# Moving VectorE's low half of the attention output from behind the last row maximum to behind the first shift of the scores

## The chip, the cores and the metric

The kernel runs on one core of a Trainium2 chip. The metric is the device time of one execution in microseconds (us), as a median over runs. The core has five engines that run beside each other, each with a queue of its own that it works off in order: TensorE (PE: matmuls, and their weight loads, shown as PEld), VectorE (DVE), ScalarE (ACT), GpSimd (POOL) and SyncE (SP, which issues DMAs). They wait for each other through semaphores.

## The reference

`x` has shape (4, 1024, 256), the context (4, 77, 256). Four layers follow each other, each added to `x`:

```python
x = x + cross_attention_0(layernorm(x), ctx)        # softmax(q k^T / 4) v, 16 heads of 16, biases
x = x + ffn_sine(layernorm(x))                      # 256 -> 1024 -> 256, sine transform, relu
x = x + cross_attention_1(ctx, layernorm(x), mask)  # the same, scores masked where mask == 0
x = x + ffn_fp4(layernorm(x))                       # gate, up, down with blockwise FP4 rounding
```

One attention, for a tile of 128 rows of `x`:

```python
q = layernorm(x) @ Wq + bq                     # (128, 256)
s = einsum(q, k)                               # (128, 16 heads, 77 keys)
p = exp((s - rowmax(s)) * scale)               # row maximum of each head
o = (p @ v) / sum(p)                           # (128, 256)
x = x + o @ Wo + bo
```

## The kernel before

The 4 x 1024 rows are T = 32 tiles of 128 rows. `attention` runs for layer l = 0 (the first attention) and l = 1 (the second), with an FFN behind each. Each attention is a software pipeline over steps i = -3 to 33, written out by hand: every engine has a function `step(i, u)` that lists its instructions for several tiles at once, and the order of these lines is the engine's order. Semaphore waits (`wait(...)`) tie the engines together. In step i the work on tile t is at these stages:

- tile i+1: layernorm result transposed (TensorE, `psQ`), copied (ScalarE, L675), query product (L753), its high half written by ScalarE (L693), its low half by VectorE (L567);
- tile i: scores (TensorE, L736, into four PSUM banks `psS[0..3]`), row maxima of each bank (`row_max`, L503), and the subtraction of the maximum (`shift`, L511);
- tile i-1: the shifted scores are transposed on TensorE in three groups of 4, 4 and 2 blocks into the one bank `psT` (L792). ScalarE takes the exponential of each group (L686). A group may overwrite `psT` only when the exponential of the group before it has ended (`prob_ready`). Then the product with the values (L814);
- tile i-2: reciprocal of the denominators (L494) and normalised output `on` (L497) on VectorE, transposed on TensorE into `psY` (`attended`, L745), high half of it rounded and copied by ScalarE (`attended_high`, L667), low half (`psY` minus the high half) by VectorE, and then the output projection on TensorE (`projected`, L762), which waits for the low half (`oT_low`). The residual (L521) adds it to `x`.

The projection multiplies split numbers, a high and a low half of both operands, so the low half `oTs[:, u, 1, :]` is needed before its first product.

TensorE's order inside a step is: scores of tile i, transposes of tile i+1, transposes of `on` of tile i-2, first group of shifted scores, query product, second group, `projected`, third group, product with the values. ScalarE's order is: copy of the transposed layernorm result (L675), `attended_high` (L667), first exponential, high half of the queries (L693), second exponential, third exponential.

In steps 5 to 28 of the first attention VectorE and GpSimd also prepare one piece of the FP4 weights of the last layer (`w4_scales`, `w4_powers`: L381 to L411 on VectorE, L400 to L424 on GpSimd). There are 24 such steps, and the second attention has none; it has instead four more matmuls per step that put the mask into the scores (L729). In step 4 of the first attention VectorE also computes small coefficients.

The line that the change moves is the low half in VectorE's `step`:

```python
wait(dve, oT_high, i - 1)
nc.vector.tensor_tensor(oTs[:, u, 1, :], psY[:, 0:KC * P], oTs[:, u, 0, :].bitcast(F32),
                        ALU.subtract).then_inc(oT_low, 1)
```

Of the kernel before, what the change touches and what calls it, by code (L numbers as in the profile page):

```python
# [53 lines left out]
def valid(t, n=T):  # L54

    return not isinstance(t, int) or 0 <= t < n


def wait(eng, sem, count):

    if not isinstance(count, int) or count > 0:
        eng.wait_ge(sem, count)
# [364 lines left out]
def attention(nc, sem, l, g):  # L427
# [5 lines left out]
    with ExitStack() as ctx:  # L433
# [42 lines left out]
        def piece_of(i):  # L476

            return i - LOOP_FROM if l == 0 and LOOP_FROM <= i < LOOP_TO else None

        def quarters_of(i):  # L480

            return {1: (0,), 2: (1,), 3: (2, 3)}.get(i, ()) if l == 0 else ()
# [4 lines left out]
        with nc.Block() as block:  # L487
            @block.vector
            def _(dve):
                def outputs(t, u):  # L490

                    wait(dve, pv_mm, t + 1)
                    o = psO[:, 0:H * VW].rearrange("p (h w) -> p h w", w=VW)
                    nc.vector.reciprocal(rden[:, u, :].unsqueeze(2), o[:, :, HD:VW]).then_inc(rden_set, 1)  # L494
                    wait(dve, rden_set, t + 1)
                    wait(dve, oT_mm, t - 1)
                    nc.vector.tensor_tensor(on[:, u, :].rearrange("p (h d) -> p h d", d=HD), o[:, :, 0:HD],  # L497
                                            rden[:, u, :].unsqueeze(2).broadcast_to([P, H, HD]),
                                            ALU.mult).then_inc(on_ready, 1)

                def row_max(t, u, j):
                    wait(dve, score_mm, NB * t + j + 1)
                    nc.vector.tensor_reduce(mx[:, u, j * BH:(j + 1) * BH],  # L503
                                            psS[j][:, 0:BH * KV].rearrange("p (h k) -> p h k", k=KV),
                                            AX.X, ALU.max).then_inc(mx_set, 1)

                def shift(t, u, j):
                    wait(dve, mx_set, NB * t + j + 1)
                    if j == 0:
                        wait(dve, prob_mm, 3 * (t - 1))  # L510
                    nc.vector.tensor_tensor(  # L511
                        shifted[:, u, 0:HK].rearrange("p (c j n k) -> p j c n k", c=KC, j=NB, n=PAIR)[:, j],
                        psS[j][:, 0:BH * KV].rearrange("p (c n k) -> p c n k", c=KC, n=PAIR),
                        mx[:, u, j * BH:(j + 1) * BH].rearrange("p (c n) -> p c n", c=KC).unsqueeze(3)
                        .broadcast_to([P, KC, PAIR, KV]),
                        ALU.subtract).then_inc(shifted_ready, 1)

                def residual(t):
                    wait(dve, y_mm, t + 1)
                    wait(dve, bias_added, t + 1)  # L520
                    nc.vector.tensor_tensor(x[:, t, :], x[:, t, :], psY[:, 0:D], ALU.add).then_inc(x_done, 1)  # L521

                def normalise(t, u):
                    wait(dve, rstd_ready, t + 1)
                    wait(dve, xT_mm, t - 1)
                    nc.vector.tensor_scalar(xhat[:, u, :], x[:, t, :], mv[:, u, 0:1], rstd[:, u, :],
                                            ALU.subtract, ALU.mult).then_inc(xhat_ready, 1)

                def step(i, u):
                    v = 1 - u  # L530
                    if valid(i - 2):
                        outputs(i - 2, u)
                    if valid(i):
                        row_max(i, u, 0)
                        row_max(i, u, 1)
                        shift(i, u, 0)
                        row_max(i, u, 2)
                        shift(i, u, 1)
                        row_max(i, u, 3)
                    if valid(i - 2):  # L540

                        wait(dve, oT_high, i - 1)
                        nc.vector.tensor_tensor(oTs[:, u, 1, :], psY[:, 0:KC * P], oTs[:, u, 0, :].bitcast(F32),  # L543
                                                ALU.subtract).then_inc(oT_low, 1)
                    if valid(i):
                        shift(i, u, 2)
                        shift(i, u, 3)
                    if piece_of(i) is not None:
                        if piece_of(i) == 0:
                            dve.wait_ge(g["in_w4"], 16)  # L550
                        w4_scales(nc, dve, g, piece_of(i), u, 0)
                    if l == 0 and i + 3 == 0:
                        dve.wait_ge(g["in_xa"], 16)
                    if l == 0 and i + 3 == 2:
                        dve.wait_ge(g["in_x0"], 16)
                    if l == 0 and i + 3 == R:
                        dve.wait_ge(g["in_x"], 16 * (B - 1))
                    if valid(i + 3):
                        nc.vector.bn_stats(st[:, v, :], x[:, i + 3, :]).then_inc(st_set, 1)
                        wait(dve, st_set, i + 4)  # L560
                    if piece_of(i) is not None:
                        w4_scales(nc, dve, g, piece_of(i), u, 1)
                    if valid(i + 1):

                        wait(dve, q_high, i + 2)
                        for k in range(KC):
                            last = nc.vector.scalar_tensor_tensor(  # L567
                                qTs[:, v, 1, k, :], psQ[:, k * P:(k + 1) * P],
                                cols[:, C_BQ + 2 * l + k:C_BQ + 2 * l + k + 1], qTs[:, v, 0, k, :].bitcast(F32),
                                ALU.add, ALU.subtract)  # L570
                        last.then_inc(q_low, 1)
                    if piece_of(i) is not None:
                        w4_scales(nc, dve, g, piece_of(i), u, 2)
                    if valid(i + 2):
                        normalise(i + 2, u)
                    if piece_of(i) is not None:
                        w4_scales(nc, dve, g, piece_of(i), u, 3)
                    if valid(i + 3):
                        nc.vector.bn_aggr(mv[:, v, :], st[:, v, :]).then_inc(mv_ready, 1)  # L579
                    for n in quarters_of(i):  # L580
                        w_low_parts(nc, dve, g, n)
                    if valid(i - 2):
                        residual(i - 2)
                    if piece_of(i) is not None:
                        w4_powers(nc, dve, g, piece_of(i), u)

                nc.vector.memset(shifted[:, 0, HK:HKP], 0.0).then_inc(pad_set, 1)
                nc.vector.memset(shifted[:, 1, HK:HKP], 0.0).then_inc(pad_set, 1)
                def masks(b):
                    part = slice(b * R * KV, (b + 1) * R * KV)  # L590
                    if b == 0:
                        dve.wait_ge(g["in_mask"], 16 * B)
                    nc.vector.tensor_scalar(mb[:, part], mask[:, part], 0.0, MASKED, ALU.is_equal, ALU.mult
                                            ).then_inc(mb_set, 1)

                if inputs:
                    inputs.angles(dve)
                step(-3, 1)
                context.key_lows(dve)
                step(-2, 0)  # L600
                if inputs:
                    inputs.pair_mask(dve)
                    dve.wait_ge(g["pairmask_set"], 1)
                context.first_keys_on_vector(dve)
                context.bias_row(dve)
                if l:
                    masks(0)
                step(-1, 1)
                for i in range(0, LAST):
                    step(i, i % 2)  # L610
                    if i == 0:
                        context.values(dve)
                    if i == 1:
                        context.projection_low(dve)
                    if i == 4 and inputs:
                        inputs.coefficients(dve)
                    if l and 0 < i < B:
                        masks(i)
# [916 lines left out]
```

## Time and profile before

| | before |
|---|---|
| median of 3 runs | 1028.1 us (1027.95 to 1029.42) |
| profiled execution, its own time | 1030.46 us |
| profiled execution, span | 1028.6 us |
| TensorE clock granted, mean | 0.963 of full |

The trace is of one execution. A row of the timeline gives the start of an instruction or of a run of like instructions (us from the span's start), its duration, engine, line and tiles; the brackets at the end give the idle time of the engine in front of it and what ended that. Instructions of one engine overlap in the timeline by some 0.1 us at their borders, so the distance between two starts is the time that one takes of its engine's queue. The first attention takes about the first quarter of the span, the second lies between about 505 and 755 us.

### The profile page before, as it was taken

Reading aid. Unit: us, or ns where it says so; the run is one execution under the profiler, and the core shown is the slowest. Engines: PE = TensorE matmul, PEld = TensorE weight load, DVE = VectorE, ACT = ScalarE, POOL = GpSimd, SP = SyncE. Lnnn points to the kernel's source line nnn. Section 1 sums busy time; section 2 is a strip of 40 time slices with the busy share of each in tenths; the row PEclk is TensorE's granted clock in tenths of the full one; section 3 lists DMA queues with packets and bytes.
Section 4 is the critical chain, followed back from the end, with each engine's and each line's share of the span. In section 5 each row is a group of like instructions: output and inputs, shape, how many; then the busy total and the mean of one; then the engine's idle time right before and its main releaser. Section 6 shows DMA issues by size and latency. Waiting matters only on the chain. (4 is left out here: it accounts for less than half of the span.)

```text
span 1028.6 us, 20339 instructions
## 1 busy us (share of the span) xinstructions
PE 931.2 (91%) x7332; PEld 819.3 (80%) x7332; DVE 832.3 (81%) x2172; ACT 487.6 (47%) x1019; POOL 466.4 (45%) x663
## 2 busy tenths in 40 slices
PE   6899999998689999998899999999868999999997
PEld 5788888887578888887688888888756888888885
DVE  5799999996399999986788787777557898898874
ACT  2534334333098888886343343333334444444442
POOL 2134545541266666664211212112026777777762
PEclk9899999999599999999999999999968999999999
DMA  9020000000000000000100000000000000000000
GB/s 344 16 94 2 2 3 2 2 2 1 0 1 1 2 1 1 1 1 4 48 2 1 2 1 2 3 1 2 1 1 1 21 1 22 21 21 21 22 21 21
DMA packets 6083, 18.32 MB, mean 18 GB/s; under 512 B 864, under 2 KB 2784, under 8 KB 5472
## 3 DMA queue, kind: packets, MB, share of 16 engines
q1 hardware_dynamic: 5264, 16.52, 4.2%
q8 instruction: 59, 0.97, 0.4%
q10 hardware_dynamic: 720, 0.50, 0.2%
q14 instruction: 40, 0.33, 0.1%
HBM read 12.83 MB, written 4.19 MB: 17 GB/s over the span
## 5 line engine op out<-in xcount | busy, mean ns | idle before, releaser
L814 PE MATMUL a_psO<-vblk,a_prob 128*128 128x51 f32 (+1 forms) x1280 | 154.1, 277 | 0.0
L814 PEld LDWEIGHTS a_psO<-vblk,a_prob 128*128 128x128 f32 x1280 | 153.8, 198 | 0.0
L1407 PE MATMUL f_psGU<-wgu,f_xTs 128*128 128x512 f32 (+1 forms) x576 | 141.3, 390 | 3.8 <-ACT f_silu L1359 2.4
L503 DVE TENSOR_REDUCE a_mx<-a_psS 128x4 f32<-128x308 f32 x256 | 115.0, 470 | 23.8 <-PE a_psS L736 23.5
L686 ACT ACTIVATE a_prob<-a_psT 128x512 f32<-128x512 f32 (+1 forms) x192 | 101.1, 526 | 68.5 <-PE a_psT L792 66.5
L675 ACT COPY a_xTs<-a_psQ 128x256 f32<-128x256 f32 x64 | 23.9, 373 | 206.6 <-PE a_psQ L745 206.6
L1407 PEld LDWEIGHTS f_psGU<-wgu,f_xTs 128*128 128x128 f32 x576 | 103.7, 192 | 19.6 <-DVE f_xTs L1171 4.4
L643 POOL TENSOR_TENSOR a_rstd<-a_mv,expo 128x1 f32<-128x1 f32 x64 | 15.3, 239 | 220.3 <-DVE a_mv L579 220.2
L511 DVE TENSOR_TENSOR a_shifted<-a_psS,a_mx 128x308 f32<-128x308 f32 x256 | 114.6, 468 | 0.0
L792 PE MATMUL a_psT<-ident,a_shifted 128*128 128x128 f32 x640 | 103.4, 276 | 9.5 <-ACT a_prob L686 9.5
L1033 PEld LDWEIGHTS s_psY<-w,s_hid 128*128 128x128 f32 x768 | 97.4, 188 | 18.1 <-POOL s_hid L951 14.3
L1033 PE MATMUL s_psY<-w,s_hid 128*128 128x256 f32 x768 | 102.3, 282 | 6.7 <-POOL s_hid L951 6.5
L1021 PE MATMUL s_psH<-s_xTs,w 128*128 128x512 f32 x384 | 102.8, 405 | 2.7 <-DVE s_xTs L932 2.0
L951 POOL TENSOR_TENSOR s_hid<-wat,s_hid 128x512 fp32r<-128x512 f32 x64 | 86.1, 1347 | 39.0 <-ACT wat L988 38.9
L1424 PE MATMUL f_psY<-wdT,f_hTs 128*128 128x256 f32 x384 | 89.7, 384 | 1.6 <-ACT f_hTs L1364 1.6
L762 PE MATMUL a_psY<-wo,a_oTs 128*128 128x256 f32 x384 | 65.6, 308 | 27.7 <-DVE a_oTs L543 27.7
L762 PEld LDWEIGHTS a_psY<-wo,a_oTs 128*128 128x128 f32 x384 | 52.1, 198 | 43.1 <-DVE a_oTs L543 43.1
L792 PEld LDWEIGHTS a_psT<-ident,a_shifted 128*128 128x128 f32 x640 | 74.7, 142 | 12.1 <-ACT a_prob L686 12.1
L1424 PEld LDWEIGHTS f_psY<-wdT,f_hTs 128*128 128x128 f32 x384 | 73.6, 192 | 13.5 <-issue 1.5
L1021 PEld LDWEIGHTS s_psH<-s_xTs,w 128*128 128x128 f32 x384 | 69.5, 193 | 16.2 <-DVE s_xTs L932 2.4
L753 PE MATMUL a_psQ<-a_xTs,wat 128*128 128x128 f32 x512 | 72.7, 286 | 1.9 <-ACT a_xTs L675 1.8
L753 PEld LDWEIGHTS a_psQ<-a_xTs,wat 128*128 128x128 f32 x512 | 63.9, 196 | 4.9 <-ACT a_xTs L675 3.4
(158 smaller groups left out, 1876.2 us busy)
## 6 DMA issues: line engine op xcount, KB each, us to landing
out_x<-x SPq DMA_DIRECT2D x8, 512.0 KB, 2.6
x<-in_x SPq DMA_DIRECT2D x3, 1024.0 KB, 13.3
w<-in_w SPq DMA_DIRECT2D x1, 2304.0 KB, 9.2
w<-in_w SPq DMA_DIRECT2D x2, 1024.0 KB, 18.0
a_mask<-in_mask SPq DMA_DIRECT2D x4, 308.0 KB, 3.9
wat<-in_att SPq DMA_DIRECT2D x1, 1024.0 KB, 22.7
x<-in_x SPq DMA_DIRECT2D x1, 768.0 KB, 9.3
wat<-in_att SPq DMA_DIRECT2D x2, 256.0 KB, 5.3
```

The costliest lines, as they stand in the source:

```text
L503: nc.vector.tensor_reduce(mx[:, u, j * BH:(j + 1) * BH], psS[j][:, 0:BH * KV].rearrange("p (h k) -> p h k", k=KV), AX.X, ALU.max).then_inc ...
L511: nc.vector.tensor_tensor(shifted[:, u, 0:HK].rearrange("p (c j n k) -> p j c n k", c=KC, j=NB, n=PAIR)[:, j], psS[j][:, 0:BH * KV].rearra ...
L686: nc.scalar.activation(prob[:, v, c0 * P:c1 * P], psT[:, 0:(c1 - c0) * P], ACT.Exp, scale=scale).then_inc(prob_ready, 1)
L753: mm = nc.tensor.matmul(psQ[:, h * P:(h + 1) * P], wat[:, k, h * P:(h + 1) * P], xTs[:, u, k * P:(k + 1) * P], start=(k == 0), stop=(k == ...
L762: mm = nc.tensor.matmul(psY[:, 0:D], oTs[:, u, a, k * P:(k + 1) * P], wo[:, b, k, :], start=(m == 0), stop=(m == len(terms) - 1))
L792: mm = nc.tensor.transpose(psT[:, (c - c0) * P:(c - c0 + 1) * P], shifted[:, v, c * P:(c + 1) * P], ident[:])
L814: mm = nc.tensor.matmul(psO[:, CH[c] * VW:(CH[c] + n) * VW], prob[:, v, c * P:(c + 1) * P], vblk[:, t // R, c * NJ * VW:(c * NJ + n) * VW] ...
L951: nc.gpsimd.tensor_tensor(hid[:, f % 4, 1, :], full[:, f % 2, :], hid[:, f % 4, 0, :].bitcast(F32), ALU.subtract).then_inc(hid_low, 1)
L1021: mm = nc.tensor.matmul(psH[f2 % 4][:], w1[:, a, k, f2 * P:(f2 + 1) * P], xTs[:, u if f + AHEAD < NF else 1 - u, b, k, :], start=(m == 0), ...
L1033: mm = nc.tensor.matmul(psY[q // 2][:, q % 2, :], hid[:, f0 % 4, a, q * P:(q + 1) * P], w2[:, b, f0, :], start=(f0 == 0 and q % 2 == 0 and ...
L1407: mm = nc.tensor.matmul(psGU[:, n0:n1], xTs[:, u, a, k * P:(k + 1) * P], wgu[:, b, k, n0:n1], start=(n == 0), stop=(n == len(TERMS) - 1))
L1424: mm = nc.tensor.matmul(psY[:, 0:D], hTs[:, 1 - u, c * P:(c + 1) * P], wdT[:, c, :], start=(c == 0), stop=(c == NF1 - 1))
```

## The change

VectorE's low half of tile i-2 (with its wait for ScalarE's high half) is issued behind the first `shift` of tile i. Before, it was issued behind the last `row_max`. Two row maxima and one shift that stood ahead of it now stand behind it. No other engine's program changes, and no instruction is added or removed.

```diff
                         row_max(i, u, 0)
                         row_max(i, u, 1)
                         shift(i, u, 0)
-                        row_max(i, u, 2)
-                        shift(i, u, 1)
-                        row_max(i, u, 3)
                     if valid(i - 2):
 
                         wait(dve, oT_high, i - 1)
                         nc.vector.tensor_tensor(oTs[:, u, 1, :], psY[:, 0:KC * P], oTs[:, u, 0, :].bitcast(F32),
                                                 ALU.subtract).then_inc(oT_low, 1)
                     if valid(i):
+                        row_max(i, u, 2)
+                        shift(i, u, 1)
+                        row_max(i, u, 3)
                         shift(i, u, 2)
                         shift(i, u, 3)
```

VectorE in a step of the first attention that prepares a weight piece, before (L503 are the row maxima, L511 the shifts, L543 the low half, L381 the first instruction of the piece):

```order
L494 RECIPROCAL a_rden<-a_psO 128x16
L497 TENSOR_TENSOR a_on<-a_psO,a_rden 128x256
L503 TENSOR_REDUCE a_mx<-a_psS 128x4 x2
L511 TENSOR_TENSOR a_shifted<-a_psS,a_mx 128x2x154
L503 TENSOR_REDUCE a_mx<-a_psS 128x4
L511 TENSOR_TENSOR a_shifted<-a_psS,a_mx 128x2x154
L503 TENSOR_REDUCE a_mx<-a_psS 128x4
L543 TENSOR_TENSOR a_oTs<-a_psY,a_oTs 128x256
L511 TENSOR_TENSOR a_shifted<-a_psS,a_mx 128x2x154 x2
L381 TENSOR_REDUCE w4scale<-w 128x12
```

The same place in the changed kernel (the low half has the line number L540 there):

```order
L494 RECIPROCAL a_rden<-a_psO 128x16
L497 TENSOR_TENSOR a_on<-a_psO,a_rden 128x256
L503 TENSOR_REDUCE a_mx<-a_psS 128x4 x2
L511 TENSOR_TENSOR a_shifted<-a_psS,a_mx 128x2x154
L540 TENSOR_TENSOR a_oTs<-a_psY,a_oTs 128x256
L503 TENSOR_REDUCE a_mx<-a_psS 128x4
L511 TENSOR_TENSOR a_shifted<-a_psS,a_mx 128x2x154
L503 TENSOR_REDUCE a_mx<-a_psS 128x4
L511 TENSOR_TENSOR a_shifted<-a_psS,a_mx 128x2x154 x2
L381 TENSOR_REDUCE w4scale<-w 128x12
```

The low half has moved up by three instructions; what stands in front of the first shift and behind the last two shifts is where it was. In the second attention the same move stands between the same neighbours, with the statistics of the next tile (L559) behind the shifts. Before:

```order
L511 TENSOR_TENSOR a_shifted<-a_psS,a_mx 128x2x154
L503 TENSOR_REDUCE a_mx<-a_psS 128x4
L543 TENSOR_TENSOR a_oTs<-a_psY,a_oTs 128x256
L511 TENSOR_TENSOR a_shifted<-a_psS,a_mx 128x2x154 x2
L559 BN_STATS a_st<-x 128x6
```

and changed:

```order
L511 TENSOR_TENSOR a_shifted<-a_psS,a_mx 128x2x154
L540 TENSOR_TENSOR a_oTs<-a_psY,a_oTs 128x256
L503 TENSOR_REDUCE a_mx<-a_psS 128x4
L511 TENSOR_TENSOR a_shifted<-a_psS,a_mx 128x2x154
L503 TENSOR_REDUCE a_mx<-a_psS 128x4
L511 TENSOR_TENSOR a_shifted<-a_psS,a_mx 128x2x154 x2
L559 BN_STATS a_st<-x 128x6
```

There too only the low half changed its place; the number of instructions in the step is the same.

## Rows read from the trace of the kernel before

**Rows 1.** The page's first part: busy time, share of the span, instructions.

```profile
PE 931.2 (91%) x7332; PEld 819.3 (80%) x7332; DVE 832.3 (81%) x2172; ACT 487.6 (47%) x1019; POOL 466.4 (45%) x663
```

**Rows 2.** Waits over the whole span: total us, times, longest.

```profile
PEld a_psY L762 <- DVE a_oTs L543: 43.1, 62, 1.3
...
DVE w4pow L408 <- POOL w4val L400: 5.7, 24, 0.2
```

**Rows 3.** Busy time by stretch: first attention's piece steps, then the second attention.

```profile
75.92:235.49 159.57, 149.82 (x1629) 138.63 (x1629) 152.02 (x540) 63.65 (x160) 81.43 (x159) 1.00 0.01 2
560.00:730.00 170.00, 160.99 (x1719) 145.08 (x1720) 131.55 (x382) 62.71 (x160) 30.83 (x64) 1.00 0.01 2
```

**Rows 4.** Timeline of one step of the second attention.

```profile
606.76 0.38 ACT L667 CAST a_oTs<-a_psY 128x256 fp32r<-128x256 f32 x1
...
607.28 0.47 DVE L503 TENSOR_REDUCE a_mx<-a_psS 128x4 f32<-128x308 f32 x1
...
607.80 0.47 PEld L792 LDWEIGHTS a_psT<-ident,a_shifted 128*128 128x128 f32 x4
...
608.44 0.41 DVE L543 TENSOR_TENSOR a_oTs<-a_psY,a_oTs 128x256 fp32r<-128x256 f32 x1
608.63 0.60 ACT L686 ACTIVATE a_prob<-a_psT 128x512 f32<-128x512 f32 x1
...
608.90 0.78 PEld L762 LDWEIGHTS a_psY<-wo,a_oTs 128*128 128x128 f32 x6 [0.63 <-DVE a_oTs L543]
...
609.62 0.25 PEld L792 LDWEIGHTS a_psT<-ident,a_shifted 128*128 128x128 f32 x2
```

**Rows 5.** Waits of VectorE for TensorE in the second attention, 560 to 730 us.

```profile
DVE a_rden L494 <- PE a_psO L814: 22.1, 22, 1.5
DVE a_mx L503 <- PE a_psS L736: 14.8, 23, 0.7
```

**Rows 6.** Timeline of one piece step of the first attention.

```profile
203.24 0.26 DVE L408 TENSOR_SCALAR w4pow<-w4val 128x192 int32<-128x192 int32 x1 [0.24 <-POOL w4val L400]
...
203.71 0.25 DVE L494 RECIPROCAL a_rden<-a_psO 128x16 f32<-128x16 f32 x1
...
204.96 0.37 ACT L667 CAST a_oTs<-a_psY 128x256 fp32r<-128x256 f32 x1
...
205.50 0.47 DVE L503 TENSOR_REDUCE a_mx<-a_psS 128x4 f32<-128x308 f32 x1
...
206.80 0.60 ACT L686 ACTIVATE a_prob<-a_psT 128x512 f32<-128x512 f32 x1
...
207.12 0.78 PEld L762 LDWEIGHTS a_psY<-wo,a_oTs 128*128 128x128 f32 x6 [0.66 <-DVE a_oTs L543]
...
207.84 0.24 PEld L792 LDWEIGHTS a_psT<-ident,a_shifted 128*128 128x128 f32 x2
...
210.80 0.25 DVE L494 RECIPROCAL a_rden<-a_psO 128x16 f32<-128x16 f32 x1
```

**Rows 7.** Timeline: first attention, behind step 29 and in step 31.

```profile
238.83 0.26 DVE L494 RECIPROCAL a_rden<-a_psO 128x16 f32<-128x16 f32 x1 [1.50 <-PE a_psO L814]
...
248.85 0.60 ACT L686 ACTIVATE a_prob<-a_psT 128x512 f32<-128x512 f32 x1 [0.74 <-PE a_psT L792]
...
250.15 0.25 PEld L792 LDWEIGHTS a_psT<-ident,a_shifted 128*128 128x128 f32 x2
```

**Rows 8.** Timeline: second attention, projection's weight loads in steps 2 and 31.

```profile
518.39 0.77 PEld L762 LDWEIGHTS a_psY<-wo,a_oTs 128*128 128x128 f32 x6 [0.63 <-DVE a_oTs L543]
...
737.14 0.77 PEld L762 LDWEIGHTS a_psY<-wo,a_oTs 128*128 128x128 f32 x6 [0.90 <-DVE a_oTs L543]
```

**Rows 9.** Timeline: product with the values in steps 31 and 32.

```profile
738.07 2.31 PEld L814 LDWEIGHTS a_psO<-vblk,a_prob 128*128 128x128 f32 x20
...
746.03 4.38 PEld L814 LDWEIGHTS a_psO<-vblk,a_prob 128*128 128x128 f32 x20
```

**Rows 10.** Timeline: first attention, step 2.

```profile
39.65 0.37 ACT L667 CAST a_oTs<-a_psY 128x256 fp32r<-128x256 f32 x1
39.76 0.47 DVE L503 TENSOR_REDUCE a_mx<-a_psS 128x4 f32<-128x308 f32 x1
```

## The prediction

> **What bounds the kernel now.** I read the busy times first, then the list of waits, then the busy times of two stretches, and last the timeline of one step in each attention. The busy times put TensorE in front, 931.2 us or 91% of the span, with VectorE at 81% [rows 1]. The waits show what this change aims at: the weight loads of the output projection waited 62 times for VectorE's low half, 43.1 us together [rows 2]. That sum is not yet a gain. It has to be asked in each attention which engine sets the length of a step.
>
> The two stretches differ. In the piece steps of the first attention VectorE is busy for 152.02 of 159.57 us and TensorE's matmuls for 149.82; in the second attention TensorE has 160.99 of 170.00 and VectorE only 131.55 [rows 3]. The timelines say the same in single waits. In a piece step VectorE runs back to back: from one reciprocal (203.71) to the next (210.80) are 7.09 us, and its only idle time is 0.24 us, which GpSimd ends, not TensorE [rows 6]; this stands 24 times in the whole span, 5.7 us [rows 2]. The reciprocal, which needs TensorE's product with the values, starts there with no idle time in front of it [rows 6]. So VectorE, with one turn through GpSimd, sets the step, and TensorE's 0.66 us of waiting is only where its slack happens to lie. In the second attention VectorE waits for TensorE twice in a step: 22.1 us over 22 steps for the product with the values, 14.8 over 23 for the scores, or 1.0 + 0.64 = 1.64 us a step [rows 5]. There TensorE sets the step, from the projection of step 2 at 518.39 to that of step 31 at 737.14: 218.75 us over 29 steps, 7.54 us each [rows 8]. Of that, 0.63 us is the wait for the low half [rows 4].
>
> **The change, part by part.** *What moves on VectorE.* The low half goes up past two row maxima and a shift. It takes the slot in which the third row maximum starts now, at 607.28 in the second attention and 205.50 in the first [rows 4, 6]. No instruction is added. One condition could keep the low half out of its new slot: ScalarE's high half must have ended. It does so at 606.76 + 0.38 = 607.14 and at 204.96 + 0.37 = 205.33 [rows 4, 6]. The handover between engines takes some 0.05 us (the low half ends at 608.44 + 0.41 = 608.85, the weight loads that wait for it start at 608.90 [rows 4]). So the high half is in hand 0.09 us early in the second attention and 0.12 us in the first. I cost the new wait at nothing. The margin is thin, and its price is a rival below. The two row maxima and the shift that come later by about 0.4 us release nobody by themselves: TensorE waits for all four shifts, and the last two keep their place in time. I cost them at nothing too; from below and above the bound is zero while the wait does not show, since the same instructions fill the same stretch.
>
> *What becomes late next on TensorE.* In the second attention the low half will end at about 607.28 + 0.41 = 607.69, long before TensorE comes to the projection. The second group of transposes starts at 607.80 and occupies the queue until 608.27, so the projection can start there and not at 608.90: 0.63 us earlier [rows 4]. But what follows is the third group of transposes, into the same PSUM bank that the second exponential reads. That exponential ends at 608.63 + 0.60 = 609.23, and it depends on nothing that moves. The third group can start at 609.23 + 0.05 = 609.28. It starts at 609.62 now [rows 4]. The gain of a step is therefore 609.62 - 609.28 = 0.34 us, and 0.29 us of the old wait come back as a wait of the third group for ScalarE. Behind the third group stands the product with the values, and with it everything that VectorE waits for; VectorE has 1.64 us to give, of which this takes 0.34 us. Steps 2 to 30 gain this: 29 x 0.34 = 9.86 us. In step 31 there is no query product, and the wait was longer, 0.90 us [rows 8]. There I use the twin in the first attention, where the second exponential ends at 248.85 + 0.60 = 249.45 and the third group starts at 250.15: 250.15 - 249.50 = 0.65 us [rows 7]. The second attention gives 10.51 us. Its last two steps (32 and 33) have no row maxima, so that nothing moves in them.
>
> *The first attention.* In the 24 piece steps TensorE's own gain would be 207.84 - (206.80 + 0.60 + 0.05) = 0.39 us [rows 6]. I count it as zero, since VectorE's chain of 7.09 us has none of TensorE in it: TensorE will then arrive early at the transposes of the normalised output, for which VectorE releases it, and wait there some 0.3 to 0.4 us. The bounds are 0 and 24 x 0.39 = 9.4 us. I take the lower end, because the row of the reciprocal has no idle time. Steps 29 and 30 have no piece, and VectorE waited 1.50 us behind step 29 [rows 7]: 2 x 0.34 = 0.68 us. Step 31 gives 0.65 us as worked out. Steps 2 to 4 I take at nothing: two of the 64 projections did not wait at all [rows 2], at the start, and step 4 has the coefficients on VectorE; were all three to gain, that would be 3 x 0.34 = 1.0 us. The first attention gives 1.33 us.
>
> *Sum.* 10.51 + 1.33 = 11.84 us. The profiled execution took 1030.46 us with a span of 1028.6, so it should go to 1018.6. The median of the runs lies 2.4 us under the profiled time; with it the forecast is 1028.1 - 11.8 = **1016.3 us**. The FFNs have no part in it: they start earlier by what the attentions save.
>
> *Uncertain sizes.* The 0.34 is a difference of starts with 0.05 us of handover in it; with 0.05 us either way over 29 steps it is 1.5 us. TensorE's clock is the other one. At the end of an attention the weight loads of one product with the values take 4.38 us where they took 2.31 a step before [rows 9], that is, the clock falls from 2.4 to 1.2 GHz as TensorE has gaps. With the gaps in other places one such product more or less may run at the lower level in each attention: 2.07 us each, 4.1 us for both, more likely against the change than for it.
>
> *A rule of the Trainium skill.* The two stretches above have different engines in front [rows 3]. The Trainium skill (Perfetto Trace Analysis, Identifying the Most-Contended Engine) says to take the engine with the highest occupancy as the one to speed up, and warns that for TensorE matmul busy time is a poor measure against weight load time. By the page's matmul figures over the whole span that is TensorE, and taking a wait off it would pay in both attentions; the sum would be 11.84 + 9.4 = 21.2 us. By the same rule applied inside the piece steps, where the rows put VectorE at 95% and the weight loads at 138.63 of 159.57 us or 87%, it pays in one only, and the sum is the 11.84 us above. The trace agrees with the second reading.
>
> **The rivals.**
>
> *More: the first attention gains too.* If VectorE's piece steps are in truth tied to TensorE by a wait that the trace does not show as idle time, each of the 24 gains 0.39 us: 1016.3 - 9.4 = 1006.9 us. For it: TensorE has the larger busy share in the page. Against it: 24 steps whose VectorE idles only for GpSimd. A cousin gives nearly the same number: if the third group is not held by the exponential, the second attention gains 29 x 0.63 + 0.90 = 19.2 us in place of 10.5, and the time is 1007.6 us. Against that stands the one bank. Together 8 in 100.
>
> *Nothing: the wait only changes its name.* The third group takes over the wait of the projection in full, because ScalarE's second exponential comes later than now, or TensorE finds another wait in front of the product with the values. Time 1028.1 us. For it: already 0.29 of 0.63 us go that way. Against it: ScalarE's instructions ahead of the exponential wait only for things of TensorE that come before the projection. 9 in 100. Between this and the forecast, with 2 to 8 us saved, 4 in 100.
>
> *Slower: the high half is late for its new place.* VectorE works in order, so if ScalarE's copy is not ready behind the first shift, two row maxima, three shifts and the whole rest of the step stand behind that wait. In the second attention the slack of 1.64 us swallows it. In the 24 piece steps every late tenth is paid, as VectorE has no slack there. The slots leave 0.12 us. In step 2 of the first attention, at the start of the pipeline, the copy ended at 39.65 + 0.37 = 40.02, and the slot is at 39.76, so that with the handover the wait would be 0.31 us [rows 10]. At that lateness everywhere the price is 24 x 0.31 = 7.4 us, and the change would still be faster, 1023.7 us. It decides from 11.84 / 24 = 0.49 us a step on; at 0.6 us the time is 1016.3 + 14.4 = 1030.7 us. Against it: the granted clock was 1.00 over the piece steps [rows 3], and the copy follows VectorE's own normalised output at a fixed distance. 5 in 100.
>
> **How the numbers follow.** The forecast has 74 in 100, the cases that save more 8, a small gain 4, nothing 9, slower 5. A difference under 0.2% (2.1 us) can't be told from no change with this kernel. Faster by more than that is 74 + 8 + 4 = 86 in 100, within it 9, slower 5. The range takes the forecast's own bounds: down 1.5 us for the size of the step and 2.1 us for one product at the higher clock, about 1012.5; up 1.5 us, 4.1 us for the clock less what is unlikely of it, about 1021. I widen the low side a little for the first steps, to 1012. The other cases stay outside; they hold the remaining 2 in 10 or so.
>
> **What would show it.** In the changed trace of the second attention the weight loads of L762 show no wait for the low half in steps 2 to 31; instead the third group of L792 waits some 0.3 us for ScalarE's L686; the distance of two steps falls from 7.54 to about 7.2 us; VectorE's waits in rows 5 fall together from 1.64 to about 1.3 us a step. In the piece steps of the first attention the distance stays 7.08 to 7.09 us, and TensorE waits 0.3 to 0.4 us for L497 in front of the transposes of L745. The low half has no idle time in front of it, but for step 2 of the first attention. The forecast is wrong if the piece steps become shorter or longer than 7.09 us, if the low half shows a wait for L667 in every step, or if the steps of the second attention stay near 7.5.

## The result and the profile after

Over six runs the changed kernel took 1019.88 us (1018.41 to 1021.4), the kernel before beside it 1030.3. The ratio is 0.9895 with a 95% interval from 0.9869 to 0.9922, or 10.8 us faster (8.0 to 13.5). The forecast was 11.8 us. The profiled execution took 1019.18 us with a span of 1017.4; before, the span was 1028.6. An execution in the slow state is left out of a ratio; there was one, of 3097.09 us, among the six of e1 below.

The waits of the changed kernel over the whole span (total us, times, longest) answer to [rows 2]:

```profile
PEld a_psT L792 <- ACT a_prob L686: 27.2, 72, 1.9
...
PEld a_psY L745 <- DVE a_on L497: 14.5, 25, 0.9
...
DVE w4pow L408 <- POOL w4val L400: 5.7, 24, 0.2
...
PEld a_psY L762 <- DVE a_oTs L540: 5.2, 4, 1.3
```

The projection's wait for the low half fell from 43.1 us in 62 waits to 5.2 us in 4, those of the last two steps of each attention. Most of it came back under two other names. In the kernel before, the same list had

```profile
PEld a_psT L792 <- ACT a_prob L686: 12.1, 12, 1.9
...
PEld a_psY L745 <- DVE a_on L497: 2.1, 3, 0.9
```

The third group of transposes waits for ScalarE 72 times in place of 12, and the transposes of the normalised output wait for VectorE 25 times in place of 3.

One step of the second attention, as in [rows 4]:

```profile
601.34 0.38 ACT L667 CAST a_oTs<-a_psY 128x256 fp32r<-128x256 f32 x1
...
601.87 0.41 DVE L540 TENSOR_TENSOR a_oTs<-a_psY,a_oTs 128x256 fp32r<-128x256 f32 x1
...
602.39 0.47 PEld L792 LDWEIGHTS a_psT<-ident,a_shifted 128*128 128x128 f32 x4
...
602.83 0.78 PEld L762 LDWEIGHTS a_psY<-wo,a_oTs 128*128 128x128 f32 x6
...
603.22 0.60 ACT L686 ACTIVATE a_prob<-a_psT 128x512 f32<-128x512 f32 x1
...
603.86 0.20 PEld L792 LDWEIGHTS a_psT<-ident,a_shifted 128*128 128x128 f32 x2 [0.26 <-ACT a_prob L686]
```

The low half starts 0.15 us after ScalarE's high half has ended and with no idle time in front. The projection follows its neighbour in TensorE's queue at once. The third group now starts 0.04 us after the second exponential has ended (603.22 + 0.60 = 603.82), after a wait of 0.26 us.

VectorE's waits for TensorE between 560 and 720 us, which answer to [rows 5]:

```profile
DVE a_mx L503 <- PE a_psS L736: 14.2, 22, 0.7
DVE a_rden L494 <- PE a_psO L814: 13.7, 22, 1.1
```

They are 1.27 us a step now in place of 1.64: TensorE still sets the step here, and VectorE has given 0.37 us of its slack. The projections of step 2 and step 31, as in [rows 8], are now 207.35 us apart, 7.15 us a step (the last one shorter than the rest):

```profile
516.89 0.77 PEld L762 LDWEIGHTS a_psY<-wo,a_oTs 128*128 128x128 f32 x6
...
724.24 0.78 PEld L762 LDWEIGHTS a_psY<-wo,a_oTs 128*128 128x128 f32 x6
```

And a piece step of the first attention, as in [rows 6]:

```profile
127.15 0.25 DVE L494 RECIPROCAL a_rden<-a_psO 128x16 f32<-128x16 f32 x1
...
127.92 0.20 PEld L745 LDWEIGHTS a_psY<-ident,a_on 128*128 128x128 f32 x2 [0.55 <-DVE a_on L497]
...
134.23 0.25 DVE L494 RECIPROCAL a_rden<-a_psO 128x16 f32<-128x16 f32 x1
134.24 0.20 PEld L745 LDWEIGHTS a_psQ<-ident,a_xhat 128*128 128x128 f32 x2
...
134.99 0.25 PEld L745 LDWEIGHTS a_psY<-ident,a_on 128*128 128x128 f32 x2 [0.55 <-DVE a_on L497]
...
135.22 0.87 PEld L792 LDWEIGHTS a_psT<-ident,a_shifted 128*128 128x128 f32 x4
```

The distance of the reciprocals is 134.23 - 127.15 = 7.08 us, as before. TensorE's idle time has moved, most of it in front of L745, and some 0.24 us of it in front of the third group. The last row is not like its siblings: four weight loads take 0.87 us where they took 0.47. The clock tells why. Busy times by stretch (PE, PEld, DVE, ACT, POOL, then the granted clock, DMA share, GB/s):

```profile
134.00:136.00 2.00, 1.69 (x19) 1.37 (x16) 1.93 (x7) 0.69 (x2) 1.92 (x4) 0.77 0.01 4
136.00:138.00 2.00, 2.00 (x12) 2.00 (x11) 2.00 (x7) 0.65 (x2) 0.92 (x2) 0.50 0.02 4
138.00:140.00 2.00, 2.00 (x16) 1.82 (x15) 1.97 (x10) 1.22 (x3) 0.00 (x0) 0.87 0.00 0
```

From the end of the wait at 134.99 until behind 138 us, TensorE ran at 1.2 GHz. The piece step took 7.94 us and the next one 7.28, together 1.06 us too long; the same came once more at 199.77. In the trace of before the granted clock was 1.00 over all piece steps [rows 3].

Where the 11.2 us of span came from, by the starts of the reciprocals (L494) in both traces:

| stretch | before | after | difference |
|---|---|---|---|
| span's start to the first reciprocal | 37.10 | 39.41 | +2.31 |
| first attention, steps 2 to 4 | 24.98 | 24.03 | -0.95 |
| its 24 piece steps | 169.96 | 172.03 | +2.07 |
| steps 29 to 31 | 20.79 | 19.29 | -1.50 |
| step 32 | 10.30 | 7.70 | -2.60 |
| up to the second attention's first reciprocal | 251.12 | 250.95 | -0.17 |
| second attention, 31 steps | 236.34 | 225.15 | -11.19 |
| the rest | 278.01 | 278.84 | +0.83 |

The second attention carries the result. The lines of the first attention's start, its step 32 and the kernel's start move between executions (step 32 took 7.26 to 10.30 us in the traces of this study, the first reciprocal came at 35.8 to 39.4 us), since the clock rises and falls there at varying times; I read nothing from them. The first and the last step of the second attention move in the same way: each took 7.1 to 7.9 us in some traces and 9.6 to 10.8 us in the others. A second trace of the changed kernel (e12 below) has 228.12 us in place of 225.15 for the second attention, with 10.06 in place of 7.15 us in its first step and the same time in the 28 steps behind it. So of the 11.19 us only what the steps between them give can be put down to the change; the table below uses those 28.

### The profile page after: what moved, and what is told of

The parts are those of the page before. It is cut to its first block and busy times, and to the rows that moved or that the text cites. A ratio compares the mean times of both kernels' runs of the same rounds, so it can differ in the third digit from the quotient of the medians.

```text
span 1017.4 us, 20339 instructions
## 1 busy us (share of the span) xinstructions
PE 931.5 (92%) x7332; PEld 818.0 (80%) x7332; DVE 832.4 (82%) x2172; ACT 487.9 (48%) x1019; POOL 465.5 (46%) x663
## 5 line engine op out<-in xcount | busy, mean ns | idle before, releaser
L503 DVE TENSOR_REDUCE a_mx<-a_psS 128x4 f32<-128x308 f32 x256 | 114.9, 470 | 24.0 <-PE a_psS L736 23.5
L792 PE MATMUL a_psT<-ident,a_shifted 128*128 128x128 f32 x640 | 108.3, 285 | 12.3 <-ACT a_prob L686 9.5
L511 DVE TENSOR_TENSOR a_shifted<-a_psS,a_mx 128x308 f32<-128x308 f32 x256 | 114.5, 468 | 0.0
L1424 PEld LDWEIGHTS f_psY<-wdT,f_hTs 128*128 128x128 f32 x384 | 73.7, 192 | 13.6 <-issue 1.5
L762 PE MATMUL a_psY<-wo,a_oTs 128*128 128x256 f32 x384 | 63.2, 302 | 3.7 <-DVE a_oTs L540 3.7
L925 DVE TENSOR_SCALAR s_turn<-s_arg 128x512 f32<-128x512 f32 x64 | 52.2, 816 | 14.7 <-ACT s_arg L1001 13.7
## 6 DMA issues: line engine op xcount, KB each, us to landing
x<-in_x SPq DMA_DIRECT2D x3, 1024.0 KB, 13.6
```

The source lines that it names most:

```text
L503: nc.vector.tensor_reduce(mx[:, u, j * BH:(j + 1) * BH], psS[j][:, 0:BH * KV].rearrange("p (h k) -> p h k", k=KV), AX.X, ALU.max).then_inc ...
L511: nc.vector.tensor_tensor(shifted[:, u, 0:HK].rearrange("p (c j n k) -> p j c n k", c=KC, j=NB, n=PAIR)[:, j], psS[j][:, 0:BH * KV].rearra ...
L762: mm = nc.tensor.matmul(psY[:, 0:D], oTs[:, u, a, k * P:(k + 1) * P], wo[:, b, k, :], start=(m == 0), stop=(m == len(terms) - 1))
L792: mm = nc.tensor.transpose(psT[:, (c - c0) * P:(c - c0 + 1) * P], shifted[:, v, c * P:(c + 1) * P], ident[:])
L1424: mm = nc.tensor.matmul(psY[:, 0:D], hTs[:, 1 - u, c * P:(c + 1) * P], wdT[:, c, :], start=(c == 0), stop=(c == NF1 - 1))
```

## The experiments

All times are against the kernel before, run beside them on the same chip. "Pieces" is the sum of the 24 piece steps, "28 steps" the distance from the second to the 30th reciprocal of the second attention, both from each kernel's own trace.

| run | ratio | 95% interval | pieces | falls of the clock in them | 28 steps |
|---|---|---|---|---|---|
| before | 1 | | 169.96 | 0 | 211.23 |
| changed | 0.9895 | 0.9869 to 0.9922 | 172.03 | 2 | 200.48 |
| e12, changed again | 0.9933 | 0.9909 to 0.9957 | 172.08 | 2 | 200.50 |
| e1, second attention only | 0.9912 | 0.9887 to 0.9937 | 169.87 | 0 | 200.50 |
| e2, first attention only | 0.9992 | 0.9965 to 1.0020 | 169.87 | 0 | 211.16 |
| e3, behind the second shift | 0.9905 | 0.9874 to 0.9935 | 170.73 | 1 | 200.57 |
| e4, behind the second maximum | 0.9989 | 0.9968 to 1.0011 | 180.15 | 5 | 200.47 |
| e5, high half late | 1.0136 | 1.0094 to 1.0177 | 191.20 | 8 | 200.09 |
| e6, changed + exponential first | 0.9883 | 0.9849 to 0.9917 | 171.95 | 2 | 198.32 |
| e8, exponential first alone | 1.0051 | 1.0022 to 1.0081 | 169.81 | 0 | 211.21 |
| e9, e1 + exponential first | 0.9875 | 0.9827 to 0.9923 | 169.82 | 0 | 198.32 |
| e10, e4 filled | 0.9959 | 0.9935 to 0.9984 | 176.15 | 0 | 200.47 |
| e11, changed filled | 0.9875 | 0.9851 to 0.9900 | 169.98 | 0 | 200.50 |
| e13, filled, exponential first | 0.9830 | 0.9796 to 0.9864 | 170.01 | 0 | 198.24 |

The repetition e12 gives 6.9 us (4.4 to 9.4) where the first runs of the same kernel gave 10.8 (8.0 to 13.5). Its 28 steps and its piece steps agree with those of the first trace to 0.05 us; what differs lies at the kernel's start and in the first and last steps of the attentions. The two gains of one kernel are 3.9 us apart, so small effects are read from the steps and not from the times.

### Which attention pays: e1 and e2

e1 takes the new place in the second attention alone, e2 in the first. e1 against the changed kernel (e2 has the numbers of l exchanged):

```diff
                         shift(i, u, 0)
+                    if valid(i) and l != 1:
+                        row_max(i, u, 2)
+                        shift(i, u, 1)
+                        row_max(i, u, 3)
                     if valid(i - 2):
...
                     if valid(i):
-                        row_max(i, u, 2)
-                        shift(i, u, 1)
-                        row_max(i, u, 3)
+                        if l == 1:
+                            row_max(i, u, 2)
+                            shift(i, u, 1)
+                            row_max(i, u, 3)
                         shift(i, u, 2)
```

> The low half stands behind the first shift in the second attention alone; the first attention keeps the old order. Theory (TensorE sets the step in the second attention, VectorE in the piece steps of the first): the second attention saves as in the changed kernel, 11 us against before, and what is lost against the changed kernel are the 1.5 us of the first attention's last three steps. In the trace the piece steps wait 0.66 us for the low half in front of the projection, not for the normalised output in front of its transposes, and the two piece steps that took 0.86 us longer in the changed trace, at a granted clock of 0.5, should not appear. Rival (the first attention gives a share like the second): half of the gain, 5 to 6 us, is lost.

> The low half stands behind the first shift in the first attention alone. Theory: 1.5 us saved by steps 29 to 31, less up to 2 us if the clock falls in piece steps again; so -1.5 to +1 us against before, not to be told from no change. The step of the second attention stays 7.54 us, that of the piece steps 7.08 us. Rival: the first attention's gain is 0.39 us in 24 piece steps, 9 us.

e1 keeps the gain of the changed kernel (0.9912 against 0.9895, the intervals overlap), and its 28 steps are the same 200.50 us. e2 cannot be told from before, and its piece steps take 169.87 us. In e2 the wait changes its place without any gain; its waits between 75 and 235 us:

```profile
PEld a_psY L750 <- DVE a_on L497: 12.6, 23, 0.6
```

That is 0.55 us in each of 23 steps. The rival by which the first attention gives its share (9.4 us) is out. The first attention of e2 is the same program as that of the changed kernel, and yet the clock did not fall in its piece steps: whether it falls differs between executions.

### What holds the step afterwards: e3, e6 and e8

e3 puts the low half behind the second shift (edit against the changed kernel):

```diff
                         shift(i, u, 0)
+                        row_max(i, u, 2)
+                        shift(i, u, 1)
                     if valid(i - 2):
...
                     if valid(i):
-                        row_max(i, u, 2)
-                        shift(i, u, 1)
                         row_max(i, u, 3)
```

> In both attentions the low half stands behind the second shift, two instructions later than in the changed kernel and one earlier than before. Theory (the third group of transposes is held by the second exponential, whatever the projection does): the low half ends some 0.27 us after TensorE comes to the projection, the projection waits that long, and the third group then waits for nothing or under 0.05 us; the step of the second attention stays 7.16 to 7.20 us and the time is that of the changed kernel, 10 to 11 us under before. Rival (the gain is proportional to how early the low half comes): a wait of 0.27 us in each of 29 steps costs 7.8 us of the 11, and 3 us under before are left.

One step of its second attention:

```profile
601.95 0.77 PEld L762 LDWEIGHTS a_psY<-wo,a_oTs 128*128 128x128 f32 x6 [0.24 <-DVE a_oTs L542]
...
602.06 0.60 ACT L686 ACTIVATE a_prob<-a_psT 128x512 f32<-128x512 f32 x1
...
602.71 0.20 PEld L792 LDWEIGHTS a_psT<-ident,a_shifted 128*128 128x128 f32 x2
```

The projection waits 0.24 us again, and the third group starts 0.05 us after the exponential has ended (602.06 + 0.60 = 602.66) with no wait shown, one too short to be listed. 28 steps take 200.57 us in place of 200.48. So 0.24 us of the wait that the change removes in a step was worth nothing: the exponential ends at the same time anyway.

e6 and e8 move the exponential itself. Both change one line in ScalarE's `step`, e6 in the changed kernel, e8 in the kernel before:

```diff
-                        if n == 0 and valid(i + 1):
+                        if n == 1 and valid(i + 1):
```

> The changed kernel, with ScalarE's second exponential in front of the high half of the queries. Theory (in the changed kernel the third group waits 0.27 us for an exponential that starts late because the high half of the queries is in front of it): the exponential can start some 0.05 us behind the second group of transposes, at 603.02 in place of 603.22, so the third group comes 0.19 us earlier, the step of the second attention falls from 7.16 to about 6.97 us, 5.5 us in all, and the wait of the third group to under 0.1 us. The piece steps keep 7.08 us. Time 16 us under before. Rival (what holds the third group is TensorE's own queue): no further gain, 11 us under before.

> The kernel before, with only ScalarE's second exponential in front of the high half of the queries; the low half stays behind the last row maximum. Theory (before the change the third group is held by the projection, and that by the low half; the exponential has 0.34 us to spare): nothing changes, the step of the second attention stays 7.54 us, the time is that of before within 1.5 us. Rival (the exponential is a cost by itself): the 5.5 us of the run with both edits come here too.

In e8 the 28 steps are unchanged (211.21). In e6 they fell from 200.48 to 198.32 us, 0.08 us a step and not the 0.19 that I expected. The row says why:

```profile
607.78 0.60 PE L792 MATMUL a_psT<-ident,a_shifted 128*128 128x128 f32 x4
...
608.11 0.77 PEld L762 LDWEIGHTS a_psY<-wo,a_oTs 128*128 128x128 f32 x6
...
608.41 0.60 ACT L686 ACTIVATE a_prob<-a_psT 128x512 f32<-128x512 f32 x1 [0.81 <-PE a_psT L792]
```

The exponential waits for the matmuls of the second group, which end at 607.78 + 0.60 = 608.38, and I had counted from the end of their weight loads, 608.14. The mechanism holds (the edit pays only behind the change, in the steps), its size was mis-read. In the time of e6 it does not show: its ratio, 0.9883, can't be told from the 0.9895 of the changed kernel, where 16 us under before had been expected.

The timed runs of e8 are another matter: 0.5% above before, where no change was expected. Its trace, of its shortest run (1030.26 us), has the piece steps and the 28 steps as before. It shows one cost, outside of them: step 3 of the first attention takes 9.48 us in place of 8.37, and so it does in e6 and e9 (9.47 us each), but not in e13, where the exponential goes first in the second attention alone (8.37 us). That is 1.1 us of some 5. What made its other runs longer no trace here shows; it stays open.

### What a late high half costs: e4 and e5

e4 puts the low half one instruction earlier than in the changed kernel, in front of the first shift; e5 is the changed kernel with `attended_high` behind the first exponential on ScalarE:

```diff
                         row_max(i, u, 1)
-                        shift(i, u, 0)
                     if valid(i - 2):
...
                     if valid(i):
+                        shift(i, u, 0)
                         row_max(i, u, 2)
```

```diff
-                    if valid(i - 2) and i != T:
-                        attended_high(i - 2, u)
                     for n in quarters_of(i):
...
+                        if n == 0 and valid(i - 2) and i != T:
+                            attended_high(i - 2, u)
                         if n == 0 and valid(i + 1):
```

> In both attentions the low half stands one instruction earlier than in the changed kernel, behind the second row maximum and in front of the first shift. Theory (VectorE pays every wait in the 24 piece steps and has slack in the second attention): its slot is then 0.26 us in front of ScalarE's high half in the first attention and 0.29 us in the second; the piece steps grow from 7.08 to 7.34 us, 6.2 us in all, the second attention keeps 7.16 us; the time is 4 to 5 us under before. Rival (ScalarE is always in time, or the wait is hidden): as the changed kernel, 11 us under before.

> The changed kernel, with ScalarE's high half issued behind its first exponential and not in front of it, so that VectorE's low half finds it late in its new place. Theory (the slower rival's mechanism, with its price by attention): the high half is seen 0.8 to 0.9 us behind the slot of the low half. In the 24 piece steps VectorE has no slack and the steps grow from 7.08 to about 7.9 us, 20 us in all; in the second attention the slack of 1.25 us swallows it and the step stays 7.16 to 7.25 us. Time 9 to 13 us above before. Rival (a wait on VectorE is hidden in both attentions): as the changed kernel, 11 us under before. Other rival (both attentions pay): 45 us above the changed kernel.

In both, the steps of the second attention are as in the changed kernel (200.47 and 200.09 us), although the low half waits there too, about 0.19 us in e4 and 0.68 us in e5: VectorE's slack takes it. In a piece step of e4 the low half waits 0.16 us, and with the overlap with its neighbour lost the step grows by 0.26 us, to 7.34. In e5 the two rows of a piece step are:

```profile
105.01 0.37 ACT L667 CAST a_oTs<-a_psY 128x256 fp32r<-128x256 f32 x1
105.41 0.42 DVE L540 TENSOR_TENSOR a_oTs<-a_psY,a_oTs 128x256 fp32r<-128x256 f32 x1 [0.71 <-ACT a_oTs L667]
```

Its piece steps are 7.87 us, and eight of them, in which the clock fell, 8.15, 21.2 us more than before in all. At 14 us above before (1.36%; 9 to 13 were expected) e5 is where the slower rival of the prediction ends: one mechanism, paid in the first attention alone. e4 was expected 4 to 5 us under before and came out 1 us under, within its interval no change. The missing 4 us are in the last columns of the table: five piece steps of 7.86 to 7.94 us, in each of which the clock fell, each followed by one of 7.57.

### Why the clock falls in piece steps: e10, e11 and e12

e10 is e4 with four more transposes in each piece step, e11 the changed kernel with two more (range 2 in place of 4), e12 the changed kernel once more:

```diff
                         wait(pe, q_low, t)
+                        for k in range(4 if piece_of(i) is not None else 0):
+                            part = slice(k % 2 * P, (k % 2 + 1) * P)
+                            nc.tensor.transpose(psQ[:, part], xhat[:, v, part], ident[:])
                         transpose_pair(psQ, xhat[:, v, :], xT_mm)
```

> The low half behind the second row maximum in both attentions, and in the piece steps of the first attention TensorE transposes the layernorm result three times in place of once (four more transposes, 0.47 us, into the same place, in front of TensorE's wait for the normalised output). Theory (the granted clock fell in every third or fourth piece step of the run without them because TensorE sat idle there in front of the transposes of the normalised output, right behind short matmuls, and not because more power was drawn): with the idle time filled the clock stays at 1.00, the longer piece steps of 7.9 and 7.57 us are gone, all are 7.34 us, and the piece steps together take some 4 us less than the 179.17 us of that run, although TensorE has more to do. Rival (the clock falls for a reason of its own): the falls stay, and the four transposes cost nothing or up to 0.47 us a step, 11 us.

> The changed kernel with two more transposes of the layernorm result in each piece step (0.24 us of TensorE, in front of its wait of 0.4 to 0.55 us). Theory: the wait in front of the transposes of the normalised output shrinks to 0.2 to 0.3 us, the two longer piece steps are gone, all are 7.08 us, 169.6 us together; time as the changed kernel or up to 2 us under it. Rival (TensorE sets the piece steps after all): 24 x 0.24 = 5.7 us slower.

> The changed kernel once more, as it is, for a second profile and more runs on one chip with the two others. Theory: one to three piece steps with a fallen clock again, at other steps than before since they are a matter of where the steps fall in time; second attention 7.16 us a step; 10 to 12 us under before. Rival (the two falls were chance of one execution, unrelated to the change): none.

The same stretch, 72 to 250 us, of e4 and then of e10:

```profile
72.00:250.00 178.00, 166.41 (x1696) 154.10 (x1694) 163.00 (x568) 68.09 (x168) 84.67 (x166) 0.95 0.01 2
```

```profile
72.00:250.00 178.00, 173.29 (x1839) 159.70 (x1837) 165.05 (x575) 69.66 (x172) 85.21 (x167) 1.00 0.01 2
```

The waits for the normalised output between 75 and 235 us, again of e4 and then of e10:

```profile
PEld a_psY L745 <- DVE a_on L497: 13.6, 17, 0.8
```

```profile
PEld a_psY L745 <- DVE a_on L497: 8.2, 22, 0.4
```

The four transposes cut the wait from 0.80 us (13.6 / 17) to 0.37 us (8.2 / 22), and in e10 every step has it, while in e4 the step behind each fall had none. With more work for TensorE the granted clock went from 0.95 to 1.00, all piece steps are 7.34 us, and together they take 4.00 us less (176.15 against 180.15). The times of the two kernels do not show this by themselves: their intervals overlap. e4's falls came in every fifth step and not every third or fourth as the expectation had it. The edit does two things at once, it gives TensorE more to do and it shortens the wait; which of the two keeps the clock up is not separated here.

In the changed kernel the same edit goes with no fall (e11, and e13 below) and piece steps of 169.98 us, where both traces of the changed kernel have two falls. But e2 has the same first attention without the edit and no fall either, so for this kernel the traces do not show that the edit removes them. e11 is faster than e12 on the same chip: 0.9875 (0.9851 to 0.9900) against 0.9933 (0.9909 to 0.9957), two intervals that do not touch (that of the changed kernel's first runs, on another chip, reaches into e11's). Of the 4.9 us between their medians, 1018.08 and 1022.96, the piece steps explain 2.1; the largest single difference between the two traces is the first step of the second attention, 7.15 against 10.06 us, which the edit does not touch.

Falls in piece steps were seen in both traces of the changed kernel, e3, e4, e5 and e6, 20 in all. Each of them began between 0.1 us before and 0.5 us after the end of TensorE's wait in front of L745. There was none in e2, which has this wait too, and none in any trace with the idle time at the projection (before, e1, e8, e9).

### The version with both findings: e9 and e13

> ScalarE's second exponential in front of the high half of the queries, and the low half behind the first shift in the second attention alone; the first attention keeps the old place. Theory (in piece steps the early low half only moves TensorE's wait in front of the transposes of the normalised output, and there the clock fell in some of them, 0.8 to 1.1 us each time): the second attention as in the run with both edits everywhere, the piece steps 7.08 us without a longer one among them, last steps 1 us slower; 15 to 16 us under before, with a tie against the run with both edits everywhere likely. Rival (the falls of the clock in piece steps have nothing to do with the place of the wait): longer piece steps appear here too.

> The changed kernel with both edits that the runs so far speak for: two more transposes of the layernorm result in each piece step of the first attention, and in the second attention ScalarE's second exponential in front of the high half of the queries. Theory: no fall of the clock in piece steps (7.08 us each), and 7.08 us for the step of the second attention in place of 7.16, 2.2 us in all; together 2 to 5 us under the changed kernel, 13 to 15 us under before. Rival (start and end of each attention, where the clock moves, swallow it): as the changed kernel with the two transposes alone, 12 to 13 us under before.

e9 is e1 with e6's line, which acts in both attentions; e13 is e11 with `if n == l` in that line, so that the exponential goes first in the second attention only. e9 did in the steps what was expected, and its 0.9875 can't be told from e6's 0.9883. e13 has the lowest ratio: 1012.75 us against 1031.04, 0.9830 (0.9796 to 0.9864), 17.5 us under before where 13 to 15 were expected. That is clear of the changed kernel's interval, but not of those of e6, e9 and e11. Of its 19.3 us of span under before, 17.0 are in the second attention (219.36 us in place of 236.34), 13.0 of them in the 28 steps; the rest lies in its first step and its last two, of which the first and the last vary between executions.

## Why the prediction was right

- *TensorE sets the step of the second attention, VectorE that of the piece steps.* Right, and shown by e1 and e2. With them the reading by the busy times of the whole span, which gave 21.2 us, is out.
- *The low half finds the high half in hand.* Right: no wait but in the steps where one was there before and step 2. The thin margin is real: one place earlier costs 0.26 us a piece step (e4).
- *0.34 us a step, held by the second exponential.* The mechanism is shown by e3 and e6. The size is 10.75 / 28 = 0.38 us. The difference is behind the third group: from its start to the product with the values are 0.17 us when it has waited (603.86 to 604.03) and 0.22 us when it follows the projection (609.62 to 609.84). Steps 2 to 30 gave 11.1 us where the term said 9.86, 1.3 us more. Step 31 gave 0.74 us where 0.65 stood.
- *Steps 29 to 31 of the first attention.* 1.50 us where 1.33 stood. Steps 3 and 4, taken at nothing, stayed at 8.37 and 7.27 us.
- *Nothing in piece steps.* Right for the step itself, 7.08 us, and wrong in its consequence: four of the 24 steps were longer, which the prediction had named as a sign of being wrong. I named the wait of 0.3 to 0.4 us that TensorE would have there (it is 0.55 us by the weight loads, 0.31 by the matmuls) and called it free. Twice in the span it took the clock with it, 2.07 us in all. The prediction had the clock as a risk, but at the end of the attentions.
- *The sum.* 10.8 us measured against 11.8: the step gave 1.3 us more, the falls took 2.1 us, and the interval of the measurement is wider than what is left. That the two come out so close is in part luck: two terms that were off cancel each other, and the repetition e12 gave 6.9 us. The mechanism does not hang on that luck, since the 28 steps have the same length in both traces. The median was 1019.88 and not 1016.3 also because the kernel before stood at 1030.3 in these runs. The range's upper side was made for a fall of the clock at the end of an attention; what fell was the clock in the piece steps.

## What to carry to other kernels

A wait at the bounding engine is worth the distance to the next thing that holds it, not its length: here 0.38 of 0.63 us, because one PSUM bank ties the next group to an exponential that nothing moved. The sum of waits over a kernel mixes stretches in which the engine has slack with those in which it has none; ask it per stretch. And a wait that is free by the clock of the program need not be free by the clock of TensorE: if it moves in front of short matmuls, look at the granted clock there.

## What the runs showed of the hardware that I had not expected

In piece steps the granted clock fell from 2.4 to 1.2 GHz although TensorE's matmuls were busy for most of the stretch: 166.41 of 178.00 us in e4, with five falls, and 152.52 of 159.57 us in the changed kernel, with two. The busy share does not tell such a stretch from one without a fall: the kernel before has 149.82 of 159.57 us and none [rows 3]. All 20 falls began at a wait that stood between two pairs of transposes, right behind the scores, of 0.5 to 1.4 us by the weight loads. The wait alone does not bring a fall in every execution (e2 has none). One fall made two steps longer by 0.8 us together in e4 and by 1.06 us in the changed kernel. Four transposes more in front of the wait, work of no use, kept the clock at 2.4 GHz in e10 and made the piece steps 4.00 us shorter for 96 transposes; one trace each of e4 and e10 shows this. After a wait TensorE passes a pair of transposes on 0.05 us faster than in a full queue (0.17 against 0.22 us from their start to the next weight load).
